# A grouped attention stage rewritten: queries in a stage of their own, fp32r products, and a slot's value piece between the transposes and the weighing

## The chip, the cores and the metric

The kernel runs on one core of one Trainium2 chip. The metric is the device time of one execution in microseconds; the time before is the median of three runs, 5122.3 us (5113.0 to 5124.93).

## What is computed

The network has four layers. Each adds to x (16 batches of 56 tokens, 256 wide) a gated cross attention over a context of 1500 rows (256 wide, one per batch), and then a gated feed-forward part. All four attentions and feed-forwards differ. The change touches one, the attention of the last layer, which the code calls x3:

```python
def _L3_xattn_ref(hidden_states, encoder_hidden_states, attention_mask, Wq, bq, Wk, bk, Wv, bv, Wo, qn_w, kn_w):
    # NH = 16 heads, NKV = 4 groups of keys and values, HD = 128
    q = (hidden_states @ Wq + bq).reshape(b, s, NH, HD).transpose(0, 2, 1, 3)
    k = (encoder_hidden_states @ Wk + bk).reshape(b, se, NKV, HD).transpose(0, 2, 1, 3)
    v = (encoder_hidden_states @ Wv + bv).reshape(b, se, NKV, HD).transpose(0, 2, 1, 3)
    k = jnp.repeat(k, GROUPS, axis=1)
    v = jnp.repeat(v, GROUPS, axis=1)
    q = _rmsnorm(q, qn_w)
    k = _rmsnorm(k, kn_w)
    scale = 1.0 / np.sqrt(HD).astype(np.float32)
    scores = jnp.einsum('bhsd,bhed->bhse', q, k) * scale
    scores = scores + attention_mask[:, None, :, :]
    probs = jax.nn.softmax(scores.astype(jnp.float32), axis=-1).astype(q.dtype)
    out = jnp.einsum('bhse,bhed->bhsd', probs, v)
    out = out.transpose(0, 2, 1, 3).reshape(b, s, NH * HD)
    return out @ Wo
```

`hidden_states` is the layer norm of x, and the result is added to x with a gate, `x + tanh(g) * out`.

## The kernel before

The program is a row of stages, x0 f0 x1 f1 x2 f2 x3 f3, which follow each other; a stage has its own buffers, semaphores and instruction streams for TensorE (PE), VectorE (DVE), ScalarE (ACT), GpSimd (POOL) and SyncE (SP, which issues the DMAs). x stays in SBUF as eight pairs of batches, each a tile of 128 rows in which a batch has 64 rows and uses 56.

x3 is `cross_attention` with `kind == 3` (L359 on). A hardware loop (L571) runs four times over four batches. What it does for them is a list of steps made by `attention_plan` (L298), and each engine walks the same list and does its part of each step; so an engine's queue is in the order of the list, and semaphores tie the engines together. The steps:

- L and Q (`queries_first`, with `product` at L622): the layer norm of a pair, its transposes, and the queries in f32, 16 records of 512 columns. QT (`queries_turned`, L655): the queries, after the bias (DVE, L830), squares (ACT, L972), sums (DVE, L837) and the scaling to unit RMS (POOL, L1057 to L1065), are transposed by head.
- K, KT and V: keys of a batch in f32 from `ctxT`, a third of the context at a time, all four groups together (512 columns); the same norm; their transposes (L678) and a copy with the norm's weight (ACT, L1019). V makes the values of 125 context rows at a time (copies L947 and L1025).
- For each slot m, a pair of heads of one batch, eight to a batch: S, scores in f32, 128 rows (two heads of 64) by three banks of 500 columns; the mask is added and the maximum taken by DVE (L859, L864); E, the exponential (ACT, L1030); N, the reciprocal of the sum and the scaling of the weights (POOL, L1075, L1077); T, twelve transposes of 125 columns (`turn`, L735) with one copy on DVE (L954) and two on ACT (L1037); W, the weighing of the values (`weigh`, L757, 12 f32 matmuls of 128 columns) with the bias on ACT (L1045).
- Y: the output projection of a pair (16 f32 matmuls), added to x by DVE (L903).

In the list T runs two slots behind S and W three. At the end of a batch the next one's keys and values are made in one go. A f32 matmul shows as two records in the trace, a fp32r one as one. x2, another attention, already has fp32r products: `split_parts` makes three of one, high times high, high times low and low times high, from operands that were split into a rounded part (`high`) and the rest (`low`).

The weights of x3 (`grouped_weights`) are loaded while f2 runs. Banks of PSUM are handed on by `Banks`: `take` on PE waits until the bank's last content was copied, `get` on a reader waits until it is filled.

Of the kernel before, what the change touches and what calls it, by code (L numbers as in the profile page):

```python
# [16 lines left out]
F32 = mybir.dt.float32  # L17
# [51 lines left out]
class Stage:  # L69


    def __init__(self, nc, ctx, name, sems, kept=""):
        self.nc, self.ctx, self.name = nc, ctx, name
        self.sem = {}
        for s in (sems + " " + kept).split():
            self.sem[s] = ctx.enter_context(nc.semaphore(f"{name}_{s}"))
        self.nums = [self.sem[s].num for s in sems.split()]
        self.kept = [self.sem[s].num for s in kept.split()]

    def sb(self, name, shape, dt=F32):  # L80
        return self.ctx.enter_context(self.nc.sbuf_tensor(f"{self.name}_{name}", shape, dt))
# [16 lines left out]
class Ahead:  # L98


    def __init__(self, nc, ctx, name, weights):
        self.st = Stage(nc, ctx, name, "weights_in")
# [15 lines left out]
    def end(self):  # L118
        self.st.reset()

# [19 lines left out]
def grouped_weights(nc, ctx, w):  # L140

    return Ahead(nc, ctx, "xa3w", {
        "wv": ([128, 2, 512], columns_of(w["L3_xattn_Wv"])), "wq": ([128, 2, 2048], columns_of(w["L3_xattn_Wq"])),
        "wk": ([128, 2, 512], columns_of(w["L3_xattn_Wk"])), "wo": ([128, HEADS, D], columns_of(w["L3_xattn_Wo"])),
        "bq_all": ([128, 2048], every_row(w["L3_xattn_bq"])), "bk_all": ([128, 512], every_row(w["L3_xattn_bk"]))})

# [144 lines left out]
ROUND_TILES = 2  # L294
RB = 2 * ROUND_TILES


def attention_plan(kind):  # L298

    if kind == 0:  # L310
        plan = [("L", 0)] + [("H", (0, j)) for j in range(3)] + [("Q", 0), ("Q2", 0), ("QH", 0), ("QB", 0)] + [("B", (0, j)) for j in range(3)]
        for m in range(8 * RB):
            plan += [("S", m)] + [("N", m - 1)] * (m >= 1) + [("W", m - 4)] * (m % 4 == 3 and m > 4)
            plan += [("T", m - 3)] * (m >= 3) + [("E", m)]
            plan += [("B", (m // 8 + 1, m % 8 - 4))] * (4 <= m % 8 <= 6 and m // 8 + 1 < RB)
            plan += [("H", (m // 8 + 1, m % 8 - 3))] * (3 <= m % 8 <= 5 and m // 8 + 1 < RB)
            if m // 16 + 1 < ROUND_TILES:
                plan += [(op, m // 16 + 1) for op, at in (("L", 7), ("Q", 8), ("Q2", 9), ("QH", 10), ("QB", 11)) if m % 16 == at]
            if m % 16 == 3 and m > 16:
                plan += [("Y", m // 16 - 1)]  # L320
        m = 8 * RB - 1
        return plan + [("N", m), ("T", m - 2), ("T", m - 1), ("T", m), ("W", m), ("Y", ROUND_TILES - 1)]
    if kind == 2:
        plan = [("H", (0, j)) for j in range(3)] + [("B", (0, j)) for j in range(3)]
        plan += [("L", 0), ("K", 0), ("Q", 0), ("V", (0, 0, 2)), ("Q2", 0), ("V", (0, 2, 4)), ("QT", 0), ("QH", 0),
                 ("V", (0, 4, 6)), ("QB", 0)]
    else:
        plan = [("L", 0), ("V", (0, 0, 4)), ("Q", 0), ("K", (0, 0)), ("QT", 0), ("K", (0, 1)), ("KT", (0, 0)), ("K", (0, 2)),
                ("KT", (0, 1)), ("V", (0, 4, 9)), ("KT", (0, 2)), ("V", (0, 9, 12))]
    for b in range(RB):  # L330
        for i in range(8):
            m = 8 * b + i
            plan += [("S", m)] + [("N", m - 1)] * (i >= 1) + [("W", m - 4)] * (kind == 2 and i == 7)
            lag = 2 if kind == 3 else 3
# [25 lines left out]

# [2980 lines left out]
```

## Time and profile before

| | us |
|---|---|
| median of three runs | 5122.3 (5113.0 to 5124.93) |
| the profiled execution | 5135.19 |
| its span in the trace | 5133.2 |
| TensorE busy in the span | 4393.5 (86%) |
| VectorE busy | 2513.1 (49%) |
| ScalarE busy | 2120.7 (41%) |
| GpSimd busy | 1610.8 (31%) |
| mean granted clock of TensorE | 0.918 |

The profiled execution is one execution, and everything that is read from the trace belongs to it; its time and its span differ by what lies before the first and after the last instruction. Busy shares are averages over eight stages that have different limits, so the stretch of x3 has to be read by itself. The granted clock is the share of full speed that TensorE was given.

### The profile page before, as it was taken

The page shows a single profiled execution, that of the slowest core. Times are in us where ns is not written, and L with a number is a line of the kernel's source. Part 1 is how long each engine was busy: PE and PEld are TensorE (multiplying, and loading weights), DVE is VectorE, ACT ScalarE, POOL GpSimd, SP SyncE. Part 2 cuts the span into 40 slices and gives each one's busy share as a digit, 9 for nine tenths or more (in the row PEclk, how much of TensorE's full clock was granted, in tenths as well). Part 3 has the DMA queues.
Part 4 walks back from the last instruction along what each step waited for, and adds up shares of the span by engine and source line. Part 5 has one row for each costly group of instructions (what it writes and reads, how often), then busy time and mean ns, then how long its engine had stood idle before and what let it go on. Part 6 is the DMA issues. An engine that isn't in the chain of part 4 may idle for free. (4 is left out here: it accounts for less than half of the span.)

```text
span 5133.2 us, 76657 instructions
## 1 busy us (share of the span) xinstructions
PE 4393.5 (86%) x28042; PEld 3114.7 (61%) x28042; DVE 2513.1 (49%) x5842; ACT 2120.7 (41%) x3793; POOL 1610.8 (31%) x1512
## 2 busy tenths in 40 slices
PE   6999348886877879779999967999999999999977
PEld 5777237765666734367777744566566566656653
DVE  6777544445757611256666653444344344434432
ACT  5777225553222211145665543444343343434421
POOL 3332013332212112111111102555455455545521
PEclk9899669998888989979998989999999999999988
DMA  3332031110000032121111110000000000000001
GB/s 118 99 98 86 24 133 48 48 48 24 1 1 1 1 110 86 32 67 41 53 36 50 38 69 17 13 25 13 13 13 13 13 13 25 13 13 13 13 13 65
DMA packets 58508, 205.37 MB, mean 40 GB/s; under 512 B 8300, under 2 KB 37740, under 8 KB 46940
## 3 DMA queue, kind: packets, MB, share of 16 engines
q1 hardware_dynamic: 58156, 200.72, 12.0%
q8 instruction: 215, 3.52, 0.3%
q14 instruction: 137, 1.12, 0.1%
HBM read 199.50 MB, written 1.20 MB: 39 GB/s over the span
## 5 line engine op out<-in xcount | busy, mean ns | idle before, releaser
L1478 DVE CUSTOM_DVE_ANT_0 xh_soft<-xh_s,xh_mask 128x500 f32<-128x500 f32 x768 | 490.9, 675 | 150.4 <-PE xh_s L1390 145.8
L1642 ACT ACTIVATE xh_probsT<-xh_t 125x512 f32<-125x512 f32 x640 | 340.3, 598 | 222.0 <-PE xh_t L1400 221.8
L1400 PEld LDWEIGHTS xh_t<-tables,xh_soft 128*125 128x125 f32 x3072 | 385.3, 198 | 68.6 <-issue 46.4
L1400 PE MATMUL xh_t<-tables,xh_soft 128*125 128x128 f32 x3072 | 420.1, 292 | 6.2 <-ACT xh_probsT L1642 4.3
L1635 ACT ACTIVATE xh_soft<-xh_soft,xh_neg_max 128x1500 f32<-128x1500 f32 x256 | 392.5, 1545 | 17.8 <-DVE xh_neg_max L1486 17.8
L1662 POOL TENSOR_TENSOR xh_ctx_low<-xh_ctxT,xh_ctx_high 128x1000 fp32r<-128x1000 f32 x96 | 223.6, 2348 | 519.0 <-ACT xh_ctx_high L1622 515.4
L859 DVE CUSTOM_DVE_ANT_0 xa_masked<-xa_s,xa_mask 128x500 f32<-128x500 f32 x384 | 260.5, 678 | 248.2 <-PE xa_s L622 240.2
L622 PE MATMUL xa_s<-xa3w_wv,xa_ctxT 128*125 128x512 f32 x768 | 346.1, 607 | 34.3 <-issue 16.0
L757 PE MATMUL xa_o<-xa_probsT,xa_values 125*128 125x128 f32 x3072 | 364.9, 276 | 6.6 <-ACT xa_outT L1045 6.6
L757 PEld LDWEIGHTS xa_o<-xa_probsT,xa_values 125*128 125x128 f32 x3072 | 353.4, 192 | 10.4 <-issue 10.4
L622 PE MATMUL xa_s<-xa3w_wk,xa_ctxT 128*125 128x512 f32 x768 | 343.2, 601 | 4.6 <-ACT xa_queries L1004 2.4
L1077 POOL TENSOR_TENSOR xa_probs<-xa_probs,xa_recip 128x1500 f32<-128x1500 f32 x128 | 343.9, 2687 | 10.1
L622 PE MATMUL xa_s<-xa_keysT,xa_queries 128*128 128x500 f32 x768 | 337.8, 583 | 0.0
L622 PEld LDWEIGHTS xa_s<-xa3w_wv,xa_ctxT 128*125 128x125 f32 x768 | 144.9, 192 | 213.1 <-issue 202.7
L972 ACT ACTIVATE xa_squares<-xa_rows 125x512 f32<-125x512 f32 (+1 forms) x224 | 140.8, 630 | 308.2 <-DVE xa_rows L830 308.2
L622 PEld LDWEIGHTS xa_s<-xa3w_wk,xa_ctxT 128*125 128x125 f32 x768 | 142.4, 190 | 173.9 <-issue 173.9
L1075 POOL TENSOR_TENSOR xa_recip<-xa_sums,minus_one 128x1 f32<-128x1 f32 x128 | 70.5, 551 | 564.1 <-ACT xa_probs L1030 564.1
L2221 POOL TENSOR_SCALAR x_k_exp<-x_k_exp 125x256 f32<-125x256 f32 x192 | 170.3, 887 | 244.8 <-ACT x_k_exp L2206 244.3
L3072 PE MATMUL f1b_s<-f_tokT,f1b_wgu 128*128 128x448 f32 x528 | 214.9, 553 | 28.3 <-PEq L95 28.3
L1065 POOL TENSOR_TENSOR xa_rows<-xa_rows,xa_square_rstd 125x512 f32<-125x512 f32 (+1 forms) x224 | 232.8, 1039 | 17.5
L1061 POOL TENSOR_TENSOR xa_square_rstd<-xa_square_sum,minus_half 125x4 f32<-125x4 f32 (+1 forms) x224 | 225.8, 1008 | 18.7
L735 PEld LDWEIGHTS xa_t<-tables,xa_probs 128*125 128x125 f32 x1536 | 184.9, 188 | 73.3 <-issue 38.9
(449 smaller groups left out, 8964.5 us busy)
## 6 DMA issues: line engine op xcount, KB each, us to landing
xh_ctxT<-ctxT SPq DMA_DIRECT2D x32, 1500.0 KB, 6.6
x_ctxT<-ctxT SPq DMA_DIRECT2D x18, 1500.0 KB, 6.3
xa_ctxT<-ctxT SPq DMA_DIRECT2D x17, 1500.0 KB, 6.5
xh_values<-ctx SPq DMA_DIRECT2D x16, 1500.0 KB
f1b_weight<-f_weights SPq DMA_DIRECT2D x32, 448.0 KB, 4.5
xh_mask<-mask_BxSxS_ff SPq DMA_DIRECT2D x32, 328.1 KB
f1b_wgu<-f_wgu SPq DMA_DIRECT2D x33, 256.0 KB, 2.7
f1b_wd<-f_wd SPq DMA_DIRECT2D x33, 128.0 KB, 2.5
```

What stands on the lines that cost most here:

```text
L622: mm = pe.matmul(bank[0:rows_out, 0:cols], lhsT, rhs, start=(n == 0), stop=(n == len(parts) - 1))
L757: mm = pe.matmul(out, values[b % 2][:, n, cols], probsT[k % len(probsT)][:, n, :], start=(n == 0), stop=(n == NKC - 1))
L859: v.tensor_tensor_reduce(masked[m % 2][:, j * THIRD:(j + 1) * THIRD], bank[:, 0:THIRD], mask[b % len(mask)][:, j * THIRD:(j + 1) * THIRD], ...
L1061: g.tensor_tensor(square_rstd[0:r, :], total, core.minus_half[0:r, :].to_broadcast([r, KV]), ALU.pow).then_inc(s["norm_ready"], 1)
L1065: g.tensor_tensor(item, item, spread(square_rstd[0:r, :], 128), ALU.mult).then_inc(s["scaled"], 1)
L1077: g.tensor_tensor(probs[m % len(probs)][:, :], probs[m % len(probs)][:, :], recip[:, m:m + 1].to_broadcast([128, SK]), ALU.mult).then_inc( ...
L1400: mm = pe.transpose(bank[0:KC, i * 128:(i + 1) * 128], soft[m % 8][:, n * KC:(n + 1) * KC], ident)
L1478: v.tensor_tensor_reduce(soft[m % 8][:, j * THIRD:(j + 1) * THIRD], bank[:, 0:THIRD], add, 1.0, -3.0e38, ALU.add, ALU.max, tops[g % 2][:, ...
L1635: a.activation(soft[m % 8][:, :], soft[m % 8][:, :], ACT.Exp, bias=neg_max[:, m % RING:m % RING + 1], accum_out=sums[:, m % RING:m % RING ...
L1642: a.activation(probsT[m % 4][:, 4 * q:4 * q + 4, :], bank[0:KC, :].rearrange("p (i n) -> p i n", i=4), ACT.Copy).then_inc(copied, 1)
L1662: g.tensor_tensor(ctx_low[b % copies][:, :, cols], ctxT[:, :, cols], whole(ctx_high[b % copies][:, :, cols]), ALU.subtract).then_inc(s["lo ...
L3072: mm = pe.matmul(bank[:, 0:HALF], wgu[i][:, k, m * 128:(m + 1) * 128], columns(k, h), start=(k == 0), stop=(k == 1))
```

## The change

Stage x3 gets new code; `cross_attention` and `attention_plan` go. The other stages stay as they are, but for the place of two weight loads.

- `grouped_queries`: before anything else, the queries of all eight pairs, in a stage of four parts (norm, rows, product, turn), skewed over the pairs: in one step an engine does turn(u), product(u+1), rows(u+2), norm(u+3). The products stay f32. The RMS norm now takes all 16 heads of a pair at once. The transposed queries are split into high and low parts and stored to a tensor in DRAM, which the loop loads again by batch and half. A store writes, for one batch, 64 columns of each head from each partition.
- `split_weights`: the high and low parts of the key and value weights.
- `grouped_attention`: all 16 batches written out, no loop. Keys, values and scores are three fp32r products. Keys and values of a batch are made in halves (two of the four groups, 256 columns) and thirds of the context; one such piece is 24 matmuls of 256 columns. A context third comes through one buffer `raw`; ACT makes its high part (H) and POOL its low part (B).
- `grouped_plan`: slots i = 0 to 3 of a batch carry the pieces of its second half, i = 4 to 7 those of the next batch's first half. In every slot TensorE does the scores, then key work, the transposes T of the slot before, then a piece of keys (first of four slots) or of values (the others), and then W of that same slot before. KS is the norm of a key piece.
- W writes 56 of the 64 columns of each of the two heads.
- The query, key and value weights are loaded during f2 as before (`early_weights`); the output weights and the key bias at the start of the new loop (`kept_weights`).

The core of the diff:

```diff
-def attention_plan(kind):
...
-def cross_attention(nc, core, kind, w, gate, ahead=None):
...
+def grouped_queries(nc, core, early, queries_dram):
...
+        plan = skewed(PAIRS, ("norm", "rows", "product", "turn"))
...
+                for u in range(PAIRS):
+                    sy.wait_ge(s["q_low"], 4 * u + 4)
+                    if u >= 2:
+                        sy.wait_ge(s[f"stored{u % 2}"], 64 * (u // 2))
+                    for i, part in enumerate((high, low)):
+                        for b in range(2):
+                            sy.dma_start(queries_dram[i, 2 * u + b].rearrange("p (h q) -> p h q", h=HEADS),
+                                         whole(part[u % 2][:, :, b * SLOT:(b + 1) * SLOT])).then_inc(s[f"stored{u % 2}"], 16)
...
+            def _(pe):
+                early.wait(pe)
+                for op, u in plan:
+                    ln = lns[u % 2]
+                    if op == "rows":
+                        pe.wait_ge(s["xn_ready"], u + 1)
+                        bank, filled = sb.take(pe, ("xnT", u))
+                        transpose_pair(pe, bank, ln.xn, ident).then_inc(filled, 1)
+                    elif op == "product":
+                        sb.copied(pe, ("xnT", u))
+                        for i in range(4):
+                            bank, filled = sb.take(pe, ("q", u, i))
+                            for k in range(2):
+                                mm = pe.matmul(bank[:, :], ln.xnT[:, k, :], wq[:, k, i * 512:(i + 1) * 512], start=(k == 0), stop=(k == 1))
+                            mm.then_inc(filled, 1)
+                    elif op == "turn":
+                        for i in range(4):
+                            pe.wait_ge(s["scaled"], 4 * u + i + 1)
+                            bank, filled = tb.take(pe, (u, i))
+                            for h in range(4):
+                                mm = pe.transpose(bank[:, h * 128:(h + 1) * 128], rows[u % 2][:, 4 * i + h, :], ident)
+                            mm.then_inc(filled, 1)
...
+            def _(g):
+                for op, u in plan:
+                    if op == "norm":
+                        layernorm_pool(g, s, lns[u % 2], core.minus_half, u)
+                    elif op == "product":
+                        total = square_sum[u % 2][:, :]
+                        g.wait_ge(s["summed"], 4 * u + 4)
+                        g.tensor_scalar(total, total, 1.0 / 128, 1e-6, ALU.mult, ALU.add).then_inc(s["norm_ready"], 1)
+                        g.wait_ge(s["norm_ready"], 2 * u + 1)
+                        if u:
+                            g.wait_ge(s["scaled"], 4 * u)
+                        g.tensor_tensor(square_rstd[:, :], total, core.minus_half[:, :].to_broadcast([128, HEADS]),
+                                        ALU.pow).then_inc(s["norm_ready"], 1)
+                        g.wait_ge(s["norm_ready"], 2 * u + 2)
+                        for i in range(4):
+                            item = rows[u % 2][:, 4 * i:4 * i + 4, :]
+                            g.tensor_tensor(item, item, spread(square_rstd[:, 4 * i:4 * i + 4], 128), ALU.mult).then_inc(s["scaled"], 1)
...
+def grouped_plan():
+    plan = [(op, (0, j)) for j in range(3) for op in "HB"]
+    for j in range(3):
+        plan += [("K", (0, 0, j)), ("KS", (0, 0, j)), ("V", (0, 0, j)), ("KT", (0, 0, j))]
+    for m in range(8 * B):
+        b, i = m // 8, m % 8
+        to, at = (b + i // 4, 1 - i // 4), i % 4
+        there = to[0] < B
+        def make(op, j):
+            return [(op, (*to, j))] * there
+        before = {0: make("K", 0), 1: make("KT", 0) + make("K", 2), 2: make("KT", 1), 3: make("KT", 2)}[at]
+        after = {0: make("K", 1), 1: make("V", 0), 2: make("V", 1), 3: make("V", 2)}[at]
+        sums = {0: make("KS", 0), 1: [], 2: [], 3: []}[at]
+        late = {0: make("KS", 1), 1: make("KS", 2), 2: [], 3: []}[at]
+        context = [(op, (b + 1, i - 2)) for op in "HB"] if 2 <= i <= 4 and b + 1 < B else []
+        plan += [("S", m), ("E", m), ("N", m)] + before + [("T", m - 1)] * (m > 0) + sums + [("Y", m // 16 - 1)] * (m % 16 == 1 and m > 16)
+        plan += after + [("W", m - 1)] * (m > 0) + late + context
+    m = 8 * B - 1
+    return plan + [("T", m), ("W", m), ("Y", PAIRS - 1)]
...
+def grouped_attention(nc, core, w, gate, early, kept):
...
+                third(0)
+                queries(0, 0)
+                queries(0, 1)
+                sy.wait_ge(s["padded"], 1)
+                for r in (0, SLOT):
+                    sy.dma_start(mask[r:r + SQ, :], w["mask"][0]).then_inc(s["mask_in"], 16)
+                kept.wait(sy)
+                for n in (1, 2):
+                    sy.wait_ge(s["low_done"], n)
+                    third(n)
+                for b in range(B - 1):
+                    sy.wait_ge(s["low_done"], 3 * b + 3)
+                    third(3 * b + 3)
+                    sy.wait_ge(s["low_done"], 3 * b + 4)
+                    third(3 * b + 4)
+                    sb.filled(sy, ("s", 8 * b + 3, 2))
+                    queries(b + 1, 0)
+                    sy.wait_ge(s["low_done"], 3 * b + 5)
+                    third(3 * b + 5)
+                    sb.filled(sy, ("s", 8 * b + 7, 2))
+                    queries(b + 1, 1)
...
+                def make_keys(b, h, j):
+                    pe.wait_ge(s["low_done"], 3 * b + j + 1)
+                    for c in range(2):
+                        bank, filled = sb.take(pe, ("k", b, h, j, c))
+                        for d in range(2):
+                            n = 4 * j + 2 * c + d
+                            at, cols = slice(n * KC, (n + 1) * KC), slice(h * 256, (h + 1) * 256)
+                            pairs = [pair for k in range(2) for pair in split_parts(
+                                ctx_high[:, k, at], ctx_low[:, k, at], parts["wk"][0][:, k, cols], parts["wk"][1][:, k, cols])]
+                            for k, (lhsT, rhs) in enumerate(pairs):
+                                mm = pe.matmul(bank[0:KC, d * 256:(d + 1) * 256], lhsT, rhs, start=(k == 0), stop=(k == len(pairs) - 1))
+                        mm.then_inc(filled, 1)
...
+                def weigh(m):
+                    b, i = m // 8, m % 8
+                    for q in range(3):
+                        tb.copied(pe, (m, q))
+                    if i % 4 == 0:
+                        for c in range(2):
+                            sb.copied(pe, ("v", b, i // 4, 2, c))
+                    bank, _ = ob.take(pe, m)
+                    out = bank[:, 0:128].rearrange("p (h q) -> p h q", h=2)[:, :, 0:SQ]
+                    for n in range(NKC):
+                        moving = probsT[m % 2][:, n, :].rearrange("p (h q) -> p h q", h=2)[:, :, 0:SQ]
+                        mm = pe.matmul(out, values[:, n, (i // 2) * 128:(i // 2 + 1) * 128], moving, start=(n == 0), stop=(n == NKC - 1))
+                    mm.then_inc(s["weighed"], 1)
...
+                    if op == "H":
+                        b, j = at
+                        cols = slice(j * THIRD, (j + 1) * THIRD)
+                        a.wait_ge(s["ctx_in"], 16 * (3 * b + j + 1))
+                        if b:
+                            sb.filled(a, ("v", b - 1, 1, j, 1))
+                        a.activation(ctx_high[:, :, cols], raw[:, :, :], ACT.Copy).then_inc(s["high_done"], 1)
...
+            def _(g):
+                for op, at in plan:
+                    if op == "B":
+                        b, j = at
+                        cols = slice(j * THIRD, (j + 1) * THIRD)
+                        g.wait_ge(s["high_done"], 3 * b + j + 1)
+                        g.tensor_tensor(ctx_low[:, :, cols], raw[:, :, :], whole(ctx_high[:, :, cols]), ALU.subtract).then_inc(s["low_done"], 1)
+                    elif op == "KS":
+                        n = key_number(*at)
+                        total = square_sum[n % 2][:, :]
+                        g.wait_ge(s["summed"], 2 * n + 2)
+                        g.tensor_scalar(total, total, 1.0 / 128, 1e-6, ALU.mult, ALU.add).then_inc(s["norm_ready"], 1)
+                        g.wait_ge(s["norm_ready"], 2 * n + 1)
+                        if n:
+                            g.wait_ge(s["scaled"], n)
+                        g.tensor_tensor(square_rstd[:, :], total, core.minus_half[0:KC, :].to_broadcast([KC, 8]), ALU.pow).then_inc(s["norm_ready"], 1)
+                        g.wait_ge(s["norm_ready"], 2 * n + 2)
+                        item = rows[n % 2][:, :, :].rearrange("p d (h e) -> p (d h) e", h=2)
+                        g.tensor_tensor(item, item, spread(square_rstd[:, :], 128), ALU.mult).then_inc(s["scaled"], 1)
+                    elif op == "N":
+                        m, r = at, at % RING
+                        g.wait_ge(s["exp_done"], m + 1)
+                        g.tensor_tensor(recip[:, r:r + 1], sums[:, r:r + 1], core.minus_one[:, 0:1], ALU.pow).then_inc(s["recip"], 1)
+                        g.wait_ge(s["recip"], m + 1)
+                        g.tensor_tensor(soft[m % 3][:, :], soft[m % 3][:, :], recip[:, r:r + 1].to_broadcast([128, SK]),
+                                        ALU.mult).then_inc(s["p_ready"], 1)
```

## Rows read from the trace of the kernel before

**Rows 1.** Stretches of x3: stretch, length, busy (count) by engine, PEclk, DMA, GB/s.

```profile
3160.00:3234.40 74.40, 58.92 (x178) 28.68 (x179) 28.06 (x46) 22.53 (x38) 36.38 (x49) 0.93 0.09 30
3234.40:4968.00 1733.60, 1673.66 (x8031) 1090.00 (x8029) 717.09 (x1573) 688.78 (x1154) 883.29 (x887) 0.99 0.04 15
3600.00:3700.00 100.00, 88.86 (x333) 50.73 (x332) 37.88 (x75) 32.70 (x55) 45.39 (x55) 0.95 0.05 17
```

**Rows 2.** Timeline, the last operation of f2 and of x3: start, length, what.

```profile
3159.72 0.48 DVE L2404 SCALAR_TENSOR_TENSOR x_all<-f_y,f_gated,x_all 128x256 f32 x1 [1.35 <-PE f_y L2370]
...
4967.52 0.48 DVE L903 SCALAR_TENSOR_TENSOR x_all<-xa_s,tanh_gates,x_all 128x256 f32 x1 [13.10 <-PE xa_s L622]
```

**Rows 3.** Groups by line, TensorE in x3: count, busy us, mean ns, idle before.

```profile
L622 PE MATMUL xa_s<-xa3w_wv,xa_ctxT 128*125 128x512 f32 x768 | 346.1, 607 | 34.3 <-issue 16.0 <-PEq L95 11.8 <-ACT xa_keysT L1019 5.0
...
L622 PE MATMUL xa_s<-xa3w_wo,xa_outT 128*128 128x256 f32 x256 | 56.9, 381 | 2.0 <-ACT xa_outT L1045 2.0
```

**Rows 4.** Timeline of TensorE, one steady slot (S, T, W) and the next start.

```profile
3251.18 2.68 PE L622 MATMUL xa_s<-xa_keysT,xa_queries 128*128 128x500 f32 x6
3253.69 1.47 PE L735 MATMUL xa_t<-tables,xa_probs 128*125 128x128 f32 x12
3255.00 2.84 PE L757 MATMUL xa_o<-xa_probsT,xa_values 125*128 125x128 f32 x24
3257.68 0.59 PE L622 MATMUL xa_s<-xa_keysT,xa_queries 128*128 128x500 f32 x1
```

**Rows 5.** Timeline of TensorE in x2: fp32r products of 500 and 256 columns.

```profile
2708.31 0.39 PE L1336 MATMUL xh_s<-xh_ctx_low,xh_wkvT_high 128*128 128x500 f32 x1
...
2711.95 0.39 PE L1336 MATMUL xh_s<-xh_ctx_high,xh_wkvT_low 128*128 128x500 f32 x1
...
2718.48 0.38 PE L1366 MATMUL xh_s<-xh_wkvT_high,xh_ctx_high 128*125 128x256 f32 x1
2718.70 0.28 PE L1366 MATMUL xh_s<-xh_wkvT_low,xh_ctx_high 128*125 128x256 f32 x1
...
2722.70 0.28 PE L1366 MATMUL xh_s<-xh_wkvT_high,xh_ctx_low 128*125 128x256 f32 x1
```

**Rows 6.** Timeline of TensorE in f1: f32 matmuls of 56 columns.

```profile
1399.64 1.89 PE L2663 MATMUL f1a_s<-f1a_keysT,f1a_queriesT 128*128 128x56 f32 x16
1401.36 0.45 PE L2653 MATMUL f1a_s<-f1a_in_T,f1w_wk 128*128 128x128 f32 x2
```

**Rows 7.** Groups by line, VectorE and ScalarE in x3.

```profile
L859 DVE CUSTOM_DVE_ANT_0 xa_masked<-xa_s,xa_mask 128x500 f32<-128x500 f32 x384 | 260.5, 678 | 248.2 <-PE xa_s L622 240.2
...
L1030 ACT ACTIVATE xa_probs<-xa_masked,xa_neg_max 128x1500 f32<-128x1500 f32 x128 | 198.0, 1547 | 60.9 <-DVE xa_neg_max L864 60.9
L1037 ACT ACTIVATE xa_probsT<-xa_t 125x512 f32<-125x512 f32 x256 | 138.8, 596 | 212.4 <-PE xa_t L735 211.8
```

**Rows 8.** Groups by line, GpSimd in x3; last, low parts elsewhere.

```profile
L1077 POOL TENSOR_TENSOR xa_probs<-xa_probs,xa_recip 128x1500 f32<-128x1500 f32 x128 | 343.9, 2687 | 10.1
L1065 POOL TENSOR_TENSOR xa_rows<-xa_rows,xa_square_rstd 125x512 f32<-125x512 f32 x192 | 199.6, 1039 | 15.0
L1061 POOL TENSOR_TENSOR xa_square_rstd<-xa_square_sum,minus_half 125x4 f32<-125x4 f32 x192 | 193.5, 1008 | 16.0
L1075 POOL TENSOR_TENSOR xa_recip<-xa_sums,minus_one 128x1 f32<-128x1 f32 x128 | 70.5, 551 | 564.1 <-ACT xa_probs L1030 564.1
L1057 POOL TENSOR_SCALAR xa_square_sum<-xa_square_sum 125x4 f32<-125x4 f32 x192 | 37.0, 193 | 107.6 <-DVE xa_square_sum L837 94.4
...
L1662 POOL TENSOR_TENSOR xh_ctx_low<-xh_ctxT,xh_ctx_high 128x1000 fp32r<-128x1000 f32 x96 | 223.6, 2348 | 519.0 <-ACT xh_ctx_high L1622 515.4
```

**Rows 9.** TensorE after waits: timeline at 3621, stretches there and in x2.

```profile
3621.36 7.14 PE L622 MATMUL xa_s<-xa3w_wv,xa_ctxT 128*125 128x512 f32 x11 [5.54 <-issue]
...
3621.40:3626.00 4.60, 4.60 (x6) 1.97 (x7) 2.16 (x6) 0.00 (x0) 0.55 (x1) 0.53 0.04 9
3626.00:3632.00 6.00, 5.26 (x14) 2.27 (x13) 0.69 (x1) 1.47 (x3) 0.00 (x0) 1.00 0.00 0
...
2594.60:2603.00 8.40, 8.11 (x59) 5.80 (x58) 4.32 (x14) 4.63 (x7) 0.00 (x0) 0.50 0.51 185
```

**Rows 10.** DMA issues (KB, us to landing); GB/s in 40 slices, 5120 to 5133.

```profile
y<-x_all SPq DMA_DIRECT2D x1, 1024.0 KB, 4.4
x_wkvT<-x_WkvT SPq DMA_DIRECT2D x1, 512.0 KB, 5.4
...
GB/s 0 0 0 0 0 0 0 0 0 0 0 0 0 0 0 0 0 0 0 0 0 0 0 0 0 0 25 0 57 350 350 350 343 347 343 350 347 343 47 0
```

More of the change, by code:

```diff
@@ L69, with __init__ @@
 class Stage:
-    def __init__(self, nc, ctx, name, sems, kept=""):
-        self.nc, self.ctx, self.name = nc, ctx, name
+    def __init__(self, nc, ctx, name, sems, kept="", side=None):
+        self.nc, self.ctx, self.name, self.side = nc, ctx, name, side
         self.sem = {}
@@ L98, with __init__ @@
 class Ahead:
-    def __init__(self, nc, ctx, name, weights):
-        self.st = Stage(nc, ctx, name, "weights_in")
+    def __init__(self, nc, ctx, name, weights, side=None):
+        self.ctx = ctx
+        self.st = Stage(nc, ctx, name, "weights_in", side=side)
         self.tensors = {k: self.st.sb(k, shape) for k, (shape, _) in weights.items()}
@@ L119, in end, with close @@
         self.st.reset()
+    def close(self):
+        self.ctx.close()
 def columns_of(source):
@@ new lines, in split_weights, with _ @@
+def split_weights(nc, early, parts):
+    with ExitStack() as ctx:
+        st = Stage(nc, ctx, "xw", "w_high w_low", side="right")
+        s = st.sem
+        with nc.Block() as block:
+            @block.scalar
+            def _(a):
+                early.wait(a)
+                for name in ("wk", "wv"):
+                    a.activation(parts[name][0][:, :, :], early.tensors[name][:, :, :], ACT.Copy).then_inc(s["w_high"], 1)
+            @block.gpsimd
+            def _(g):
+                for n, name in enumerate(("wk", "wv")):
+                    g.wait_ge(s["w_high"], n + 1)
+                    g.tensor_tensor(parts[name][1][:, :, :], early.tensors[name][:, :, :], whole(parts[name][0][:, :, :]),
+                                    ALU.subtract).then_inc(s["w_low"], 1)
+        st.reset()
@@ L3279, in program @@
         with ExitStack() as after:
-            ahead = grouped_weights(nc, after, A) if "x3" in stages else None
+            kept = kept_weights(nc, after, A) if "x3" in stages else None
+            before = after.enter_context(ExitStack())
+            early = early_weights(nc, before, A) if "x3" in stages else None
             if "f2" in stages:
-                ffn_ternary(nc, core, {"fc": A["L2_ffn_W_fc"], "proj": A["L2_ffn_W_proj"]}, 6, ahead)
+                ffn_ternary(nc, core, {"fc": A["L2_ffn_W_fc"], "proj": A["L2_ffn_W_proj"]}, 6, early)
             if "x3" in stages:
-                cross_attention(nc, core, 3, {"ctxT": A["ctxT"], "mask": A["mask_1xSxS2_ff0"]}, 3, ahead)
+                grouped_attention(nc, core, {"ctxT": A["ctxT"], "mask": A["mask_1xSxS2_ff0"]}, 3, early, kept)
         if "f3" in stages:
```

1057 lines of the change are left out of this document (345 added, 712 removed).

## The prediction

> **What bounds the kernel now.** Only the fourth attention stage (x3) is touched, so I read the busy table by stretches first: from the first score on, TensorE is busy 1673.66 of 1733.60 us at a mean clock of 0.99, while the others are at about half. [rows 1] That stretch is bound by TensorE. The stretch before it, 74.4 us, is filling. The loop boundaries are the only leak (88.86 of 100 us around 3600). From the end of the last operation of the stage ahead (3159.72 + 0.48) to that of this one (4967.52 + 0.48) the stage takes 1807.8 us. [rows 2] So a change pays where it takes columns from TensorE, and it costs where it puts TensorE behind something. The grouped table of TensorE's lines gives 346.1 us for the values over 16 batches, 21.6 each, the keys being the same work, and 56.9 / 8 = 7.1 for an output projection. [rows 3] A steady slot lasts 6.50: scores 2.51, transposes 1.31, weighing 2.68. [rows 4] Six score records in 2.51 are 0.418 each, and 0.428 at 512 columns.
>
> **New prices on TensorE.** Three fp32r products take the place of an f32 one of two records. The trace has them in x2: 500 columns every (2711.95 - 2708.31) / 16 = 0.2275 us, 256 columns every (2722.70 - 2718.70) / 34 = 0.1176. [rows 5] Scores: 9 x 0.2275 = 2.05 (was 2.51). A key or value piece: 24 x 0.1176 = 2.82; 12 pieces are 33.9 a batch where 43 stood. Key transposes of one piece, 8 records at the transposes' 0.109: 0.87. Weighing now writes 112 of 128 columns: 16 f32 records of 56 columns take 1401.36 - 1399.64 = 1.72, 0.108 each, no less than those of 128. [rows 6] So I take 24 x 0.109 = 2.62; in proportion it would be 2.30 (42 us less over 128 slots). Each change of group costs 0.06, between 0 and the 0.10 that the first step in rows 5 is longer than the others: with 42 groups a batch, 40 us either way at most.
>
> **The walk through a half batch.** Per four slots TensorE does S, K0, T, K1, W | S, KT0, K2, T, V0, W | S, KT1, T, V1, W | S, KT2, T, V2, W. With the switches these are 11.9, 12.85 and twice 9.95. In the last two W finds its transposed weights late: ScalarE does the exponentials (1.55) first, then two key copies, then two copies of 0.60, and VectorE its own after the keys' low parts; copies are ready 7.65 after the slot's start, TensorE at 7.27, so both become 10.3. [rows 7] A half is 45.35, a batch 90.7. The value piece (2.82) is what hides the rest of these copies; without it W would wait some 3 us in each such slot. The loop: 15 x 90.7 + 45.4 + four last slots of 6.6 (scores, T, W and its wait) - 3.9 (the first slot has neither T nor W) = 1428. Seven output projections inside it: 49. The last T, W and projection: 15.
>
> **The wait that it adds.** GpSimd's queue is the place to look. The order in slot i=4 is: reciprocal and scaling of the weights, key norm KS0, KS1, then the low part of the next batch's last context third. TensorE's K2 in slot i=5 waits for that third. The prices: reciprocal 0.55, scaling 2.69; a key norm now takes 8 columns through the power and 1024 through the multiply. The power costs 0.55 for one column and 1.01 for four, so 0.152 more each and 1.61 for eight; 1024 columns cost twice 1.04 or 0.68 of 2.69 (1.83), I take 2.0; with the 0.19 and the gaps a unit is 4.04. A low third is 2.35. [rows 8] The exponentials of the slot end at 5.1, the scaling at 8.4, KS0 at 12.5, KS1 at 16.5, the third at 18.9. TensorE comes to K2 at 11.9 + 2.05 + 0.87 + 0.1 = 14.9 and waits 4.0. Behind K2 stand T, V0 and W, and nothing later makes it up, as TensorE is the bound. Its clock pays too: after the 5.5 us idle before 3621.4 the next 4.6 us ran at 0.53, about half, so 2.0 more. [rows 9] 6.0 x 15 batches = 90. Bounds: nothing (see the first rival) and, with x2's clock, 165. For the other half (slots i=0..3) the context is there already.
>
> **The query stage.** All queries are made ahead, in a stage of their own. On TensorE a step is turn(u), product(u+1), rows(u+2), and turn(u) waits for everything between product(u) and its scaled rows, so nothing overlaps that chain: after the last product 0.2, one bias add and four reductions at 0.68 (rows 7: VectorE's operation on as many columns), 3.6 in all; on GpSimd 0.28, a power over 16 columns 0.55 + 15 x 0.152 = 2.84, four multiplies of 1.04, with gaps 11.3; the last four transposes end at 12.0. The power is between 1.01 (no more than for four columns: 15 us less over the stage) and 4 x 1.01 (10 more). A product is 16 x 0.428 = 6.9 at full clock and 13.8 at half. TensorE comes to it from a wait of some 11 us; if it regains its clock after about 4 us of work, as in rows 9, the step is 12.0 + 8.9 = 20.9, with 18.9 and 25.8 as its ends. 8 x 20.9 + 4.4 for the first rows + 1.7 for the start + 10 for the last store = 183 us. The old stage hid all but the first of these queries beside its loop and paid TensorE time for them alone.
>
> **The stores.** Each pair stores 2 MB, in pieces of 256 B (64 columns of one head), and a step hides it if it lands within a step. The nearest rows: 1 MB in pieces of 1 KB took 4.4 us, and 512 KB 5.4 with its start. [rows 10] At the bandwidth of the first, 2 MB take 9. If a piece of 256 B costs as much time as one of 1 KB, there are 8192 of them against 1024: 8 x 4.4 = 35, or, without the start of each and at the 350 GB/s that the 1 KB pieces reached, 8 x 3.0 = 24. I take under 20.9, hidden, and 10 for the last one alone (6 to 35).
> The Trainium skill ("DMA: Bandwidth & Descriptors", Specifications) asks for at least 512 B in a transfer for line rate, which speaks against these stores; no row here has a store of 256 B alone. By it the stores outlast the step, and the sum is that of the second rival; by the bandwidth of rows 10 it stays as it is.
>
> **The rest.** Splitting the key and value weights and three stage ends: 10 (5 to 20). Filling the new loop: three context thirds through one buffer, each 5.4 + 1.02 + 2.35 and latencies, 29 together, the 2 MB of output weights asked for ahead of the first; then for each third K, its norm, KT in series, 2.82 + 2.4 + 4.04 + 0.87, about 10: 58 together (45 to 70).
>
> **The sum**, in the profiled execution's measure: 183 + 10 + 58 + 1428 + 49 + 90 + 15 = 1833 against 1807.8, so +25 on 5135.19, 5160. The loop gains 152 (1582 for 1734), the way to its first score loses 177 (251 for 74). The profiled execution is 12.9 above the median of the runs, 5122.3; on the median's footing I forecast 5147.
>
> **The rivals.**
> 1. No wait before K2 (faster). It is gone when the third's low part is done by 14.9, that is, when the two norms take 4.1 together, as they would if the new unit cost half of my price, or when slots are longer than I think before K2. For it: GpSimd was busy only half of the old stretch. Against: its queue is in order and all four durations are from rows. 90 less: 5057. The loop's gain stays, the query stage's loss too.
> 2. Query stage worse (slower): stores at 24 to 35 us a pair set its step instead of the chain, or every product runs at half clock (25.8). 8 x 4.9 = 39 more for the clock; for stores of 24, 8 x 3.5 and 15 for the last, 43; for stores of 35, 113: 5186 to 5260, and I put it at the lower end. For it: 256-B pieces, and TensorE mostly idle in this stage. Against: the clock came back within 5 us in rows 9.
> 3. The clock stays low longer after each wait. In x2 it was still 0.50 through 8.40 us after a quiet stretch (rows 9); 7 us lost for each wait where I count 2: 75 more, 5222.
> 4. The change doesn't do what it says: the value piece doesn't cover the copies. If ScalarE's order makes them a further microsecond late in the last two slots of a half: 64 slots, 64 more, 5211. If it covers them fully, 25 less.
>
> **How the numbers follow.** Chances: forecast 0.42, rival 1 0.22, rival 2 0.18, rival 3 0.08, rival 4 0.10. Below 0.2% (about 10 us) this kernel's runs can't tell a change from none. The forecast's own spread is from 5100 to 5190, by the switches, the power, the filling; about 0.09 of it lies under 5112 and 0.09 within 10 us of the old median. With rival 1's 0.22 and 0.02 of others that is 0.33 faster, 0.12 the same, 0.55 slower. The range takes in rival 1 (5057) with half of the cheaper weighing, down to 5035, and all the others' own values, up to 5230; what is left out is rival 1 with several other savings on one side, and the slowest stores or two of the slower rivals together on the other.
>
> **What would show it.** Right: scores near 2.05, pieces near 2.82; before each K2 of slot i=5 an idle of about 4 us on TensorE that ends with GpSimd's low part, 15 times; a query stage of about 183 us in which TensorE's waits end with GpSimd's multiplies; a first score about 250 us after the stage's start; from there to the end about 1582. Wrong: no idle before K2, a query step far from 21 us, the store queue as what TensorE or ScalarE waits for there, W waiting more than half a microsecond for copies, or a granted clock well below 1 in the loop.

## The result and the profile after

The changed kernel takes 5141.01 us (median of 7 runs, 5124.81 to 5152.69), the kernel before 5119.27 in the runs beside it: a ratio of 1.0045 (95% interval 1.003 to 1.0059), so slower by some 22 us, less than half a per cent. The forecast was 5147 and 25 more. The profiled execution took 5152.69 us, the longest of the seven (the forecast for it was 5160), and spans 5150.9.

Spans are compared inside the stage here. The code ahead of the stage is the same in all the changed kernels, and yet f2 ended anywhere from 3134.8 to 3158.1 us after the start in their traces; 23 us of a span's difference may come from there.

First the two operations between which the stage lies, in the timeline of the kernel after (start, length, what):

```profile
3153.51 0.48 DVE L2152 SCALAR_TENSOR_TENSOR x_all<-f_y,f_gated,x_all 128x256 f32 x1 [1.34 <-PE f_y L2118]
...
4988.73 0.48 DVE L1323 SCALAR_TENSOR_TENSOR x_all<-xg_s,tanh_gates,x_all 128x256 f32<-128x256 f32 x1 [10.82 <-PE xg_s L1259]
```

From 3153.99 to 4989.21 are 1835.2 us, where rows 2 gave 1807.8: 27 more, all of it in this stage. Then its stretches: the query stage, the end of it with the split weights and the first loads, the filling of the loop, the loop (stretch, length, busy by engine, PEclk):

```profile
3154.00:3313.60 159.60, 96.72 (x272) 50.54 (x272) 75.18 (x136) 44.08 (x71) 61.96 (x56) 0.77 0.36 92
3313.60:3348.70 35.10, 0.04 (x2) 0.04 (x1) 4.34 (x4) 3.73 (x4) 6.93 (x3) 0.50 0.62 187
3348.70:3396.00 47.30, 27.93 (x169) 26.95 (x170) 14.21 (x21) 11.38 (x17) 15.85 (x11) 0.72 0.12 36
3396.00:4989.20 1593.20, 1489.53 (x11224) 1417.31 (x11224) 776.22 (x1683) 696.27 (x1150) 866.78 (x580) 0.97 0.08 25
```

Against [rows 1] the loop is 140 shorter (1593 for 1734) and the way to the first score 168 longer (242 for 74). That way is where TensorE does little: 97 of 160 us, nothing in 35, 28 of 47.

TensorE's waits in the stage, grouped by what ended them (sum, times, longest):

```profile
PE xg_s L1179 <- POOL xg_ctx_low L1391: 92.6, 16, 35.1
PE xg_o L1237 <- DVE xg_probsT L1319: 33.6, 63, 1.0
PE xq_t L938 <- POOL xq_rows L1023: 33.0, 8, 7.8
PE xq_s L228 <- DVE xq_xn L212: 26.1, 7, 3.7
```

The first row is K2's wait: 35.1 once while filling, and 57.5 over the 15 batches, 3.83 each. This is GpSimd's queue ahead of one of them (timeline): weights of slot 4, the two key norms, the low part; and below it TensorE's K2, T, value piece and weighing.

```profile
3646.71 0.55 POOL L1407 TENSOR_TENSOR xg_recip<-xg_sums,minus_one 128x1 f32<-128x1 f32 x1 [1.09 <-ACT xg_soft L1364]
3647.34 2.69 POOL L1409 TENSOR_TENSOR xg_soft<-xg_soft,xg_recip 128x1500 f32<-128x1500 f32 x1
3650.11 0.20 POOL L1396 TENSOR_SCALAR xg_square_sum<-xg_square_sum 125x8 f32<-125x8 f32 x1
3650.39 1.65 POOL L1400 TENSOR_TENSOR xg_square_rstd<-xg_square_sum,minus_half 125x8 f32<-125x8 f32 x1
3652.12 1.90 POOL L1403 TENSOR_TENSOR xg_rows<-xg_rows,xg_square_rstd 125x1024 f32<-125x1024 f32 x1
...
3656.11 1.90 POOL L1403 TENSOR_TENSOR xg_rows<-xg_rows,xg_square_rstd 125x1024 f32<-125x1024 f32 x1
3657.96 2.30 POOL L1391 TENSOR_TENSOR xg_ctx_low<-xg_raw,xg_ctx_high 128x1000 fp32r<-128x1000 f32 x1
```

```profile
3660.32 0.41 PE L1179 MATMUL xg_s<-xgw_wk_high,xg_ctx_high 128*125 128x256 f32 x1 [3.77 <-POOL xg_ctx_low L1391]
...
3664.77 1.47 PE L1223 MATMUL xg_t<-tables,xg_soft 128*125 128x128 f32 x12
3666.00 0.36 PE L1191 MATMUL xg_s<-xgw_wv_high,xg_ctx_high 128*125 128x256 f32 x1
...
3668.91 2.83 PE L1237 MATMUL xg_o<-xg_probsT,xg_values 125*128 125x112 f32 x24
3671.50 0.47 PE L1214 MATMUL xg_s<-xg_keys_high,xg_queries_high 128*128 128x500 f32 x1
```

GpSimd's queue has no gap from 3646.71 on, and K2 on TensorE starts as it ends. The next batch's K2 starts at 3756.36, 96.04 later; the forecast's batch was 90.7 + 6.0 = 96.7. K2 itself took 4.45 instead of 2.82: the granted clock was 0.54 from 3660.3 to 3663.5 and 1.00 from 3664.8 on, so its first records ran at half clock, as in [rows 9].

### The profile page after: what moved, and what is told of

Same layout as the page of the kernel before. It is cut to its first block and busy times, and to the rows that moved or that the text cites. A ratio compares the mean times of both kernels' runs of the same rounds, so it can differ in the third digit from the quotient of the medians.

```text
span 5150.9 us, 83520 instructions
## 1 busy us (share of the span) xinstructions
PE 4262.6 (83%) x31498; PEld 3480.6 (68%) x31498; DVE 2640.4 (51%) x6067; ACT 2165.0 (42%) x3843; POOL 1645.5 (32%) x1226
## 5 line engine op out<-in xcount | busy, mean ns | idle before, releaser
L1309 DVE CUSTOM_DVE_ANT_0 xg_soft<-xg_s,xg_mask 128x500 f32<-128x500 f32 x384 | 247.1, 677 | 369.5 <-PE xg_s L1214 369.5
L1237 PE MATMUL xg_o<-xg_probsT,xg_values 125*128 125x112 f32 x3072 | 371.8, 278 | 43.4 <-DVE xg_probsT L1319 33.6
L1237 PEld LDWEIGHTS xg_o<-xg_probsT,xg_values 125*128 125x128 f32 x3072 | 357.8, 194 | 55.2 <-issue 44.8
L1409 POOL TENSOR_TENSOR xg_soft<-xg_soft,xg_recip 128x1500 f32<-128x1500 f32 x128 | 344.2, 2689 | 10.0
L1179 PE MATMUL xg_s<-xgw_wk_high,xg_ctx_high 128*125 128x256 f32 x768 | 236.4, 308 | 92.6 <-POOL xg_ctx_low L1391 92.6
L1179 PE MATMUL xg_s<-xgw_wk_low,xg_ctx_high 128*125 128x256 f32 x768 | 230.0, 300 | 0.0
L1179 PE MATMUL xg_s<-xgw_wk_high,xg_ctx_low 128*125 128x256 f32 x768 | 229.7, 299 | 0.0
L1191 PE MATMUL xg_s<-xgw_wv_high,xg_ctx_high 128*125 128x256 f32 x768 | 223.7, 291 | 0.0
L1191 PE MATMUL xg_s<-xgw_wv_low,xg_ctx_high 128*125 128x256 f32 x768 | 215.6, 281 | 0.0
L1191 PE MATMUL xg_s<-xgw_wv_high,xg_ctx_low 128*125 128x256 f32 x768 | 215.5, 281 | 0.0
```

Source lines behind the costliest of these rows:

```text
L1179: mm = pe.matmul(bank[0:KC, d * 256:(d + 1) * 256], lhsT, rhs, start=(k == 0), stop=(k == len(pairs) - 1))
L1191: mm = pe.matmul(bank[0:KC, d * 256:(d + 1) * 256], lhsT, rhs, start=(k == 0), stop=(k == len(pairs) - 1))
L1237: mm = pe.matmul(out, values[:, n, (i // 2) * 128:(i // 2 + 1) * 128], moving, start=(n == 0), stop=(n == NKC - 1))
L1309: v.tensor_tensor_reduce(soft[m % 3][:, cols], bank[:, 0:THIRD], mask[:, cols], 1.0, -3.0e38, ALU.add, ALU.max, tops[m % 2][:, j:j + 1]).t ...
L1409: g.tensor_tensor(soft[m % 3][:, :], soft[m % 3][:, :], recip[:, r:r + 1].to_broadcast([128, SK]), ALU.mult).then_inc(s["p_ready"], 1)
```

## The experiments

All are edits of the changed kernel, and the ratios are to the kernel before; a comparison with the changed kernel is one of ratios (1.0045).

**The context one slot earlier.**

```diff
-        context = [(op, (b + 1, i - 2)) for op in "HB"] if 2 <= i <= 4 and b + 1 < B else []
+        context = [(op, (b + 1, i - 1)) for op in "HB"] if 1 <= i <= 3 and b + 1 < B else []
```

> The high and low parts of the next batch's context thirds are moved one slot earlier (slots i=1..3 instead of 2..4), so that GpSimd's queue has the last third done before the two key norms of slot 4. Theory (the loop's loss is this queue order): TensorE's waits for the low part go from 57.5 us in the 15 slots to near 0, and with them some 1.8 us of half clock each, 27: 85 us less than the changed kernel, about 5056, faster than the kernel before. Rival (the wait only moves, to the context's transfer through its single buffer, to the copies ahead of the weighing or to the key norms): under 30 us less, 5111 or more, with a new wait of 2 us or more in each batch.

Measured: 5055.19, ratio 0.9881 (0.9848 to 0.9913). The wait for the low part is left only in the filling:

```profile
PE xg_s L1179 <- POOL xg_ctx_low L1391: 34.6, 1, 34.6
PE xg_o L1237 <- DVE xg_probsT L1319: 34.1, 63, 1.0
```

The loop falls from 1593 to 1507, 86 less, of which 57.5 is the wait and the rest half clock: TensorE's busy time for the same 11224 records falls by 29 (1489.53 to 1460.48), and the granted clock from 3392 to 4870 is 1.00 to two digits. The theory holds, the wait went nowhere else.

**Only the order in GpSimd's queue of slot 4.**

```diff
-        plan += after + [("W", m - 1)] * (m > 0) + late + context
+        plan += after + [("W", m - 1)] * (m > 0) + (context + late if i == 4 else late + context)
```

> Only GpSimd's order in slot i=4 changes (and ScalarE's not): the low part of the third goes before the second key norm, same work in the same slot. Theory: the low part then starts when its high part is made, after the weighing's bias at some 13.6 into the slot, and ends near 15.9, where TensorE wants it at 14.9: the wait falls from 3.8 to about 1.1, no clock is lost, so about 41 + 27 = 68 us less, 5073 (5060 to 5095). Rival: the wait is for the transfer or the high part in any order: no change, about 5141; or the delayed second norm then holds up the key transposes of slot 6: a new wait there of 1 us or more.

Measured: 5075.92, ratio 0.9929 (0.9904 to 0.9953). The wait is 47.8 - 34.6 = 13.2 in 15 batches, 0.88 each:

```profile
PE xg_s L1179 <- POOL xg_ctx_low L1391: 47.8, 16, 34.6
```

No other wait of TensorE grew by more than half a microsecond. Same work, same slot, another order: 65 us. So it was the place in the queue, and not GpSimd's load or the transfer.

**The value piece behind the weighing.**

```diff
-        plan += after + [("W", m - 1)] * (m > 0) + late + context
+        weighing = [("W", m - 1)] * (m > 0)
+        plan += (weighing + after if at else after + weighing) + late + context
```

> The value piece goes behind the weighing instead of between the transposes and the weighing (slots 1 to 3 of each half; the key piece of slot 0 stays). Theory (the piece covers the copies of the transposed weights): W then waits about 0.9 in slot 1 and 3.3 in slots 2 and 3 where it waited 0.5, 6.5 more in each of 31 halves: 200 us more, 5340, and up to 60 more where these waits lower the clock. Rival (the order of the two is worth little, as another engine ends last anyway): within 30 us of 5141.

Measured: 5499.24, ratio 1.0751 (1.071 to 1.0793): 358 more, where 200 to 260 were expected. The waits:

```profile
PE xg_o L1238 <- DVE xg_probsT L1320: 210.1, 63, 3.7
PE xg_o L1238 <- ACT xg_probsT L1372: 47.2, 28, 2.6
```

They sum to 257.3, against 43.4 in the changed kernel: 214 more, as expected. The other 144 is the clock, which I had put at 60 at most: the granted clock of the loop is 0.89 for 0.97, TensorE's busy time for the same 11224 records rises by 148 (1489.53 to 1637.19), and a weighing behind a wait looks like this (timeline of TensorE):

```profile
3662.52 5.43 PE L1238 MATMUL xg_o<-xg_probsT,xg_values 125*128 125x112 f32 x24 [3.35 <-DVE xg_probsT L1320]
...
3678.80 4.53 PE L1238 MATMUL xg_o<-xg_probsT,xg_values 125*128 125x112 f32 x24 [3.36 <-DVE xg_probsT L1320]
...
3695.01 2.83 PE L1238 MATMUL xg_o<-xg_probsT,xg_values 125*128 125x112 f32 x24
```

A wait of 3.35 cost up to 2.6 more in the 24 records behind it. The piece's place between T and W is worth both.

**The product ahead of the turn, in the query stage.**

```diff
-        plan = skewed(PAIRS, ("norm", "rows", "product", "turn"))
+        plan = []
+        for slot in range(PAIRS + 3):
+            for op, lag in (("product", 2), ("turn", 3), ("rows", 1), ("norm", 0)):
+                plan += [(op, slot - lag)] * (0 <= slot - lag < PAIRS)
```

> In the query stage the order of one step becomes product(u+1), turn(u), rows(u+2), norm(u+3) on all engines, instead of turn(u) first. Theory (the step is the chain of one pair in series, since turn(u) stands ahead of the next product): the chain now overlaps the next product, and a step falls from 19.2 to about 12 (VectorE's own work there is about 10, product and turn on TensorE 8.7), 7 steps of it: about 50 less, 5091 (5075 to 5105). Rival (the stores of 2 MB in 256-byte pieces set the step): 16 or more, under 25 us less, with VectorE or ScalarE waiting for a store.

Measured: 5137.77, ratio 1.0034 (1.0017 to 1.0051), 5 to 6 less and not told from none. In the traces the query stage with the split weights, from the end of f2 to VectorE's first operation in the loop's stage, takes 172.6 where the changed kernel's takes 180.6: 8 less of the 50 forecast, so the theory failed. First the changed kernel's step on TensorE, from product to product 19.06 (timeline):

```profile
3178.83 7.24 PE L931 MATMUL xq_s<-xqw_wq,xq_xnT 128*128 128x512 f32 x16
3189.81 0.48 PE L228 MATMUL xq_s<-tables,xq_xn 128*128 128x128 f32 x1 [3.73 <-DVE xq_xn L212]
3190.08 0.42 PE L229 MATMUL xq_s<-tables,xq_xn 128*128 128x128 f32 x1
3193.98 4.11 PE L938 MATMUL xq_t<-tables,xq_rows 128*128 128x128 f32 x16 [3.49 <-POOL xq_rows L1023]
3197.89 7.95 PE L931 MATMUL xq_s<-xqw_wq,xq_xnT 128*128 128x512 f32 x16
```

and the step with the product first, 17.7 here and 18.3 in the mean of six steps (TensorE, then VectorE in the same step):

```profile
3182.29 8.51 PE L934 MATMUL xq_s<-xqw_wq,xq_xnT 128*128 128x512 f32 x16 [0.47 <-ACT xq_xnT L990]
3190.64 1.47 PE L941 MATMUL xq_t<-tables,xq_rows 128*128 128x128 f32 x12
3194.96 0.75 PE L941 MATMUL xq_t<-tables,xq_rows 128*128 128x128 f32 x4 [2.85 <-DVE xq_low L975]
3198.84 0.48 PE L228 MATMUL xq_s<-tables,xq_xn 128*128 128x128 f32 x1 [3.14 <-DVE xq_xn L212]
...
3200.01 9.88 PE L934 MATMUL xq_s<-xqw_wq,xq_xnT 128*128 128x512 f32 x16 [0.47 <-ACT xq_xnT L990]
```

```profile
3192.88 1.28 DVE L968 TENSOR_REDUCE xq_square_sum<-xq_squares 128x4 f32<-128x512 f32 x2 [0.16 <-ACT xq_squares L997]
3194.07 0.74 DVE L975 SCALAR_TENSOR_TENSOR xq_low<-xq_t,xq_qn_w,xq_high 128x512 fp32r<-128x512 f32 x1
...
3197.93 0.86 DVE L212 TENSOR_SCALAR xq_xn<-xq_x,xq_mv,xq_rstd 128x256 f32<-128x256 f32 x1 [0.22 <-DVE xq_low L975]
```

The turn no longer waits for GpSimd's multiplies, but the next product wants rows that VectorE normalises behind four low parts of the turned queries. One wait took the other's place, and the products ran longer, 9.1 in the mean for 7.5.

**The norm ahead of the low parts.** Rows are made two steps ahead of their product, and VectorE walks the list in its own order:

```diff
+            step = {op: [(op, slot - lag)] * (0 <= slot - lag < PAIRS)
+                    for op, lag in (("product", 3), ("turn", 4), ("rows", 1), ("norm", 0))}
+            plan += step["product"] + step["turn"] + step["rows"] + step["norm"]
+            vector_plan += step["product"] + step["rows"] + step["turn"] + step["norm"]
```

> The query stage as in the product-first run, and the rows of a pair are now normalised and transposed two steps ahead of its product; VectorE does that norm before the low parts of the turned queries instead of behind them. Theory (in the product-first run the step stayed at 17.7 to 19 because the next product waited for a norm that stood behind four low parts in VectorE's queue): from a product's end 3.6 for the sums, 0.8 norm, some 1 for the first low part and the last transposes, 0.9 rows: the next product starts 6.5 after the last one ended, a step of 13.4 to 14.5, about 5 less over each of 7 steps: 35 less than the changed kernel, 5106 (5095 to 5118). Rival A (VectorE's own work of some 12 and the squares that wait for its sums bind it at 17 or more): under 15 less. Rival B (the stores bind it): 16 or more with a wait for a store.

Measured: 5112.86, ratio 0.9982 (0.9968 to 0.9996). Steps of 14.1:

```profile
3180.76 8.61 PE L936 MATMUL xq_s<-xqw_wq,xq_xnT 128*128 128x512 f32 x16
...
3194.89 8.38 PE L936 MATMUL xq_s<-xqw_wq,xq_xnT 128*128 128x512 f32 x16
...
3208.99 8.15 PE L936 MATMUL xq_s<-xqw_wq,xq_xnT 128*128 128x512 f32 x16
```

From the end of f2 to the first score it is 204.3 instead of 241.9. Of these 38, 35 are in the query stage (145.8 for 180.6), as forecast; the other 3 are in the filling, which the edit doesn't touch: from its first squares to the first score the granted clock was 0.77 for 0.70. So the query stage was bound by the orders of its queues; the stores of 256-byte pieces did not bind it, since only the last one was waited for (4.1). This edit puts the product first, makes the rows a step earlier and puts VectorE's norm ahead. The first alone was worth 8; the other two were not run apart, so which of them gave the rest isn't shown.

**All 128 columns in the weighing.**

```diff
-                    out = bank[:, 0:128].rearrange("p (h q) -> p h q", h=2)[:, :, 0:SQ]
+                    out = bank[:, 0:128]
...
-                        moving = probsT[m % 2][:, n, :].rearrange("p (h q) -> p h q", h=2)[:, :, 0:SQ]
+                        moving = probsT[m % 2][:, n, :]
```

> The weighing writes all 128 columns again instead of 112. Theory (an f32 record costs the same at 56 and at 128 columns, so it does between them): no change within 8 us of the changed kernel's 5141. Rival (cost goes with the columns, 0.30 a slot): 128 slots, 38 more, 5179.

Measured: 5150.34, ratio 1.0051 (1.0028 to 1.0075), the changed kernel's within the intervals. Busy time of the weighing's group, first at 112 (after), then at 128:

```profile
L1237 PE MATMUL xg_o<-xg_probsT,xg_values 125*128 125x112 f32 x3072 | 371.8, 278 | 43.4 <-DVE xg_probsT L1319 33.6 <-ACT xg_probsT L1371 9.8
```

```profile
L1237 PE MATMUL xg_o<-xg_probsT,xg_values 125*128 125x128 f32 x3072 | 373.6, 279 | 43.6 <-DVE xg_probsT L1319 33.8 <-ACT xg_probsT L1371 9.8
```

The 16 columns left out are worth 1.8 us in all, not 38.

**Versions that beat both.** The earlier context and the query order together with a third edit, by which SyncE asks for the first third and the queries ahead of the output weights:

> Three edits together: the context's parts one slot earlier (85 less measured alone), the query order (35 less forecast), and the output weights asked for behind the first context third and the queries instead of ahead of them (the third was asked for 7.6 us before it landed where 4.0 was the median; 3 to 6 less). Theory (three separate places of the chain, so their gains add): 123 less than the changed kernel, 5018 (5005 to 5035), faster than the kernel before by 2%. Rival (they share a wait): 30 or more short of that sum.

Measured: 5025.6, ratio 0.9815 (0.9786 to 0.9844), 118 less than the changed kernel where 123 were expected. The way to the first score is 209.9, longer than the 204.3 of the query order alone. VectorE waits 13.9 for the key bias, but that isn't what the way waits for (VectorE, then two of ScalarE):

```profile
3302.85 1.29 DVE L1280 TENSOR_TENSOR xg_rows<-xg_s,xgk_bk_all 125x512 f32<-125x512 f32 x2 [13.86 <-DMA xgk_bk_all<-L_xattn_bk]
```

```profile
3314.05 1.04 ACT L1339 ACTIVATE xg_ctx_high<-xg_raw 128x1000 fp32r<-128x1000 f32 x1 [6.24 <-DMA xg_raw<-ctxT]
3315.00 1.13 ACT L1346 ACTIVATE xg_squares<-xg_rows 125x512 f32<-125x512 f32 x2
```

The rows have their bias by 3304.14, and their squares start 11 us later, since in ScalarE's queue they stand behind the high part of the last context third. That third is late: SyncE asks for the second and third only when the weights have landed, and here these were asked for later. Without the third edit:

> The context one slot earlier and the query order together, without the third edit of the run before (the output weights stay ahead of the first third). Theory (that edit cost time: the key bias then landed 13.9 after VectorE was ready for it, and the second and third context thirds stood behind the wait for the weights in SyncE's queue, so the way from the end of f2 to the first score was 209.9 where the query order alone had 204.3): the way is 204 and the loop 1507 as in the run with the earlier context; 5 to 6 less than the three edits together, 5020 (5010 to 5030). Rival (the third edit was neutral, and 204.3 was chance): the way stays near 210 here too.

Measured: 5030.42, ratio 0.9816 (0.9783 to 0.9849). The way is 204.3 and the loop 1505, as expected; in the runs' times the two can't be told apart. From VectorE's first operation in the loop's stage to the squares it is 26.6, for 29.5 with the third edit: this is the late third. The rest of the 5.6 lies behind the squares, 31.9 at a granted clock of 0.77 for 34.7 at 0.70. That isn't the edit: the changed kernel has these loads in the same order as this run, and has 34.7 at 0.70 there too. With the first third alone ahead, and the wait for the weights behind the other two:

> As the run with two edits, and the first context third alone goes ahead of the output weights and the key bias, with the wait for these behind the second and third thirds in SyncE's queue. Theory (the order of the first loads is a small term of the filling): the first key product starts 3 to 4 earlier, the bias comes at most 3 late, so the way to the first score is 199 to 203; 5017, no difference in the time that runs can show. Rival: the bias is late by 10 again, and the way is 208 or more.

Measured: 5027.56, ratio 0.9809 (0.9779 to 0.984). The way is 206.5, between the two theories, and neither names the cause. The first key product came 6.8 earlier after the end of f2, and the bias was not what held it up:

```profile
3314.36 0.69 DVE L1280 TENSOR_TENSOR xg_rows<-xg_s,xgk_bk_all 125x512 f32<-125x512 f32 x1 [7.14 <-DMA xgk_bk_all<-L_xattn_bk]
```

VectorE was idle for 7.1, but the products that it adds the bias to started at 3311.14, and in the run with two edits it adds the bias 3.0 after that, so the bias was some 0.2 late. The squares again stand behind the last third and start 26.1 after the stage's first operation, 0.5 earlier than without this edit; then 34.7 pass to the first score, at 0.70 again. So the order of these loads was worth half a microsecond, and the clock cost 2.9.

## Why the prediction was right

By its terms, forecast and measured in the profiled execution: the query stage to its last store 183, and 173.5 (to 3327.47, where the weights' split begins); the split 10, and 6.7; the filling 58, and 61.7; the loop 1582, and 1593. The sum 1833, and 1835. The sum came closer than its terms: the query stage and the split were 13 shorter than forecast, the filling and the loop 15 longer, and that these cancel is luck.

- **The price of TensorE's work**: right. K2 to K2 is 96.0 to 97.6, 96.8 in the mean of seven, for 96.7, and 103.0 for 103.8 where a projection lies between; the scores step to the transposes in 3673.62 - 3671.50 = 2.12 for 2.05 and a switch.
- **The wait before K2**: right in its place, cause and size (3.83 for 4.0; the norms 1.65 + 1.90 for 1.61 + 2.0). The two experiments on the queue's order show the cause, and 28 us beside the wait in the first of them is the clock, for which I had 2.0 x 15 = 30.
- **The value piece as cover**: right, and undoing it shows it. W's waits on VectorE are 33.6 for the 22 that the walk gave (0.35 in two slots of each half): 0.53 each, just over the half microsecond that the prediction names as a sign of being wrong, but the batches are no longer for it.
- **The last four slots**: mis-sized. They have no value piece, so W waits 2.4 in each, and three of the four weighings behind that wait ran mostly at half clock, at 0.61 in the mean. The four took 39.7 where 4 x 6.6 = 26.4 was counted, although the prediction itself says that W waits some 3 us without the piece. These 13 are more than the 11 by which the loop is over. One of them (timeline of TensorE, from T to T):

```profile
4957.22 1.47 PE L1223 MATMUL xg_t<-tables,xg_soft 128*125 128x128 f32 x12
4961.14 4.47 PE L1237 MATMUL xg_o<-xg_probsT,xg_values 125*128 125x112 f32 x24 [2.45 <-ACT xg_probsT L1371]
4967.50 1.47 PE L1223 MATMUL xg_t<-tables,xg_soft 128*125 128x128 f32 x12
```

- **The query stage**: the cause was half right. The chain from the end of a product to the end of its turn is 12.0 in the step shown (3198.09 - 3186.07), as forecast. The product was mis-sized: behind the first pair it ran in 7.0 to 8.2, nearer to the 6.9 of full clock than to the 8.9 that I took, so the step is 19.2 and not 20.9. I had TensorE come to it from one wait of some 11 us; in the trace it waits 3.7 and 3.5, with the transposes of two rows between them and the turn behind. Whether this is why the clock stayed up was not tested. And the chain of one pair is one bound of the step but not the only one: with the product first, VectorE's queue order held it at 18.3, so that freeing the first alone gave next to nothing.
- **The rivals**: the first needed norms at half my price, and they were not. The stores (second rival) landed 5 to 7 us after their issue at the median, and only the last was waited for, 4.2 us by SyncE: they ran below the rate of the 1 KB stores, but a pair's 2 MB took about 10 of the step's 19.2. Two sums of that rival are off: stores of 24 are 3.1 over the step and not 3.5, and the 113 for stores of 35 leaves out the last store, 25 more. The clock (third) came back within 4 us of work behind K2's wait. Of the fourth rival's microsecond more in W's wait, 0.2 came.

Not settled: the rest of the execution was 10 us shorter than before by the spans, within what f2's end moves from run to run; 6 of them lie before the stage (f2 ended at 3153.99 for 3160.20). The forecast had put the rest at no change.

## What to carry to other kernels

Where one engine is the bound, a slot plan has to be read from the queue of every other: add up what stands ahead of the one operation that the bound engine needs next, and put that first; in this loop the order alone was worth 65 us, and the same work one slot earlier 86. A stage that is a chain through four engines can have two queue orders that bind at nearly the same step, so that curing one shows almost nothing until both are cured (8 us alone, 35 together). A wait of 3 to 4 us on TensorE cost half to two thirds as much again by the clock behind it in these runs (29 beside 57.5, and 148 beside 214). And an engine's idle time ahead of a late operand isn't how late the operand was for the chain: look whether the next reader was ready.

## What the runs showed of the hardware

The 256-byte stores ran at up to 216 GB/s where the 1 KB ones in [rows 10] reached 350: so a quarter of the size cost well under twice the time per byte, and 2 MB took about 10 us. Whether the size of the pieces alone set this rate was not tested. This is the rate of the query stage, 40 slices from 3160 to 3310:

```profile
GB/s 0 0 0 0 0 28 214 215 102 0 23 215 214 111 0 0 180 210 173 0 0 197 214 149 0 0 157 215 187 0 0 90 214 215 44 2 102 216 215 29
```

GpSimd's power went on at the slope of [rows 8] to 16 columns: 1.65 us for 8 and 2.90 for 16, where the slope gives 1.61 and 2.84.
